# TensorE's wait before the gate and up products of a mixture of experts, split in two

## The chip, the cores and the metric

The kernel runs on one core of one Trainium2 chip, as one program. The metric is the device time of one execution in microseconds. Engines are named as the profile names them: PE is TensorE's products, PEld its weight loads, DVE is VectorE, ACT is ScalarE, POOL is GpSimd, SP is SyncE, which here only issues transfers. Each engine works through a queue of its own, in order, and the engines meet over semaphores.

## The reference

Two layers work on x of 4 x 1024 x 128 (float32). Layer 0 is a linear attention and a mixture of 8 experts with a capacity of 640 tokens each; layer 1 is a causal attention with cosine weights (16 heads of 64) and a mixture of 16 routed and 2 shared experts. What matters here is the mixture of layer 0:

```
disp = tokens scattered to [8 experts, 640 slots, 128]
h    = silu(disp @ W1) * (disp @ W2)        # gate and up, 128 -> 512, per expert
out  = h @ W3                               # down, 512 -> 128, per expert
y    = the two chosen experts' rows of each token, weighted and added
```

## The kernel before, in words

The program has four stages: layer 0's attention and routing, layer 0's experts, layer 1's attention, layer 1's mixture. The change is in the second.

**Half blocks.** For each expert the hidden width of 512 is cut into four blocks m of 128, and the 640 slots into two halves of 320. A half block is one (m, half); an expert has 8, numbered n = 0 to 7, and through all experts j = 8e + n, 0 to 63. For each half block TensorE makes a gate product and an up product, each [128, 320] from three matmuls in a row (weights and slots are split into a high and a low part of type fp32r, and high x high, high x low and low x high are added in PSUM). They go to banks 2(n % 2) and 2(n % 2) + 1: gate to bank 0 or 2, up to bank 1 or 3. So a bank is used again two half blocks on.

**Who reads the banks.** ScalarE waits for the gate product (`e_gate`), and also for VectorE's product of half block j - 2 (it overwrites that half of `e_sg`), reads the gate bank through SiLU, writes `e_sg` and counts the semaphore `e_sg` up. VectorE waits for `e_sg` and `e_up`, reads the up bank, multiplies the two into `e_hs` and counts `e_h` up. In the last expert the result goes to the tile that the profile calls sb_h.

**The order on TensorE** is written out in `experts_tensor` (L1195): for an expert e of 1 to 6 it is half blocks 0 and 1; the transposes of expert e + 1's slots (`slots_tensor`, L1177); the down product of expert e - 1 (`down_tensor0`, L1252, 20 products in 40 passes); half blocks 2 to 7. Expert 0 has the transposes before its half block 4 and no down product; expert 7 has the down products of ten single tiles in three groups (`tiles_tensor`, L1273). Before a half block with half = 0 TensorE waits for the split weights (`e_ws`), before half block 0 for the transposed slots (`e_xT`).

**The order beside it.** ScalarE copies the down products out (L1329, L1330, then a drain) ahead of the activation of half block 2, and rounds the next expert's weights to the high part (L1288) behind odd half blocks. VectorE makes the low parts (L1294), the split of the turned slots (L1367, L1375) behind half block 1 (5 in expert 0), and the lists of rows (L1382 to L1387) at the end of an expert. GpSimd scatters each expert's outputs to DRAM (L1163). SyncE loads weights and slots two experts ahead: `experts_sync` issues W3 (L1098) when the down product of the expert before is done, and right behind it W1, W2 (L1093, L1094) and the slots (L1103).

Of the kernel before, what the change touches and what calls it, by code (L numbers as in the profile page):

```python
# [76 lines left out]
class Kernel:  # L77
# [1117 lines left out]
    def experts_tensor(self):  # L1195
        pe, S, bank = self.pe, self.S, self.bank
        three = ((0, 0), (0, 1), (1, 0))
        self.first_slots_tensor()
        for e in range(E0):
            i, last = e % 2, e == E0 - 1  # L1200
            for n, (m, half) in enumerate(self.jobs(e)):
                j = 2 * NB * e + n
                if not last and n == 2 * self.slots_at(e):
                    self.slots_tensor(e + 1)
                if last:
                    self.tiles_tensor(n)
                elif e and n == 2:
                    self.down_tensor0(e - 1)
                if half == 0:
                    pe.wait_ge(S["e_ws"], NB * e + m + 1)  # L1210
                if n == 0 or (e == 0 and n == 1):
                    pe.wait_ge(S["e_xT"], e + 2 if e else half + 1)
                cols = slice(half * HC, (half + 1) * HC)
                pe.wait_ge(S["e_h"], max(0, j - 1))
                for w, name in enumerate(("e_gate", "e_up")):
                    for k, (wp, xp) in enumerate(three):
                        ins = pe.matmul(bank[2 * (n % 2) + w][:, 0:HC], self.ews[:, i, wp, w, m * P:(m + 1) * P],  # L1217
                                        self.xeT[:, i, xp, cols], start=(k == 0), stop=(k == 2))
                    ins.then_inc(S[name], 1)
        self.tiles_tensor(2 * NB)  # L1220
# [1479 lines left out]
```

## Time and profile before

| what | us |
|---|---|
| runs of the kernel, median of 3 | 871.64 |
| lowest and highest of them | 871.23, 872.01 |
| profiled execution, its span | 873.5 |
| PE busy in the span | 817.3 (94%) |
| DVE, ACT, POOL busy | 614.8, 432.0, 394.9 |

The span reaches from the first to the last instruction of one profiled execution. A row of the order of time reads: start, length, engine, line, operation, out<-in, count, and in brackets how long the engine had been idle before it and for whom. Matmuls overlap, so the length of a row of many is not their sum. Times of start are from the span's beginning; the experts' stage lies between about 166 and 272 us.

### The profile page before, as it was taken

What the parts mean: (1) busy time and instruction counts of PE and PEld (TensorE: products, weight loads), DVE (VectorE), ACT (ScalarE), POOL (GpSimd) and SP (SyncE); (2) the same over time, 40 slices, a digit from 0 to 9 for tenths busy, and PEclk for the clock granted to TensorE, in tenths of its full rate; (3) what the DMA queues carried; (4) which work ended last, traced back from release to release, by engine and by line L of the source; (5) the groups of instructions that cost most, each with busy time, mean ns of one, the idle gap of its engine ahead of it and who ended that gap; (6) DMA issues with size and microseconds to landing.
All of it is one profiled execution on the core that took longest, in us unless ns stands there. A gap on an engine that the chain in (4) does not pass through costs nothing.

```text
span 873.5 us, 32577 instructions
## 1 busy us (share of the span) xinstructions
PE 817.3 (94%) x13678; PEld 704.8 (81%) x13678; DVE 614.8 (70%) x1775; ACT 432.0 (49%) x944; POOL 394.9 (45%) x399
## 2 busy tenths in 40 slices
PE   6999985699997899999999999999999999999998
PEld 5777854588996688888888888888888888878887
DVE  7888885575664775675777785876876776858875
ACT  6556532544343755555556465565564464433322
POOL 4358877224454653644545654457442342500000
PEclk9999995599998999999999999999999999999999
DMA  9714100524322100000100100100000000027761
GB/s 292 252 63 160 37 26 11 175 76 128 94 76 84 31 27 4 27 3 3 51 3 3 29 3 3 53 3 4 4 3 3 5 3 3 4 57 148 157 125 40
DMA packets 67905, 49.66 MB, mean 57 GB/s; under 512 B 5298, under 2 KB 62785, under 8 KB 67377
## 3 DMA queue, kind: packets, MB, share of 16 engines
q1 hardware_dynamic: 64288, 42.41, 18.1%
q0 software_dynamic: 3328, 5.16, 1.8%
q8 instruction: 109, 1.79, 0.8%
q14 instruction: 36, 0.29, 0.1%
q10 hardware_dynamic: 144, 0.02, 0.0%
HBM read 33.20 MB, written 16.10 MB: 56 GB/s over the span
## 4 chain that ended last, share of the span: by engine, by line
PE 78%; DVE 7%; issue 5%; POOL 4%; ACT 3%; DMA 2%; SPq 0%; ACTq 0%; POOLq 0%; DVEq 0%
PE psum L1531 11%; PE psum L1636 8%; PE psum L1663 7%; PE psum L1614 7%; PE psum L2294 5%; PE psum L1217 5%; PE psum L1566 5%; PE psum L1595 5%; PE psum L2312 4%; PE psum L1651 3%; PE psum L1577 3%; PE psum L1549 3%; PE psum L1252 3%; POOL disp L307 3%; DMA sb_e_x<-disp 1%
## 5 line engine op out<-in xcount | busy, mean ns | idle before, releaser
L2192 POOL TENSOR_TENSOR sb_a_qr<-sb_h,sb_a_csq 128x512 f32<-128x512 f32 x64 | 81.4, 1294 | 113.8 <-PE psum L1636 107.9
L2192 POOL TENSOR_TENSOR sb_a_qr<-sb_a_qp,sb_a_csq 128x512 f32<-128x512 f32 (+1 forms) x64 | 72.2, 1151 | 116.4 <-PE psum L1636 116.4
L1531 PE MATMUL psum<-sb_wkv,sb_a_hs 128*128 128x512 f32 x384 | 122.5, 428 | 1.0 <-ACT sb_a_hs L1982 0.7
L1790 ACT ACTIVATE sb_a_vr<-sb_a_va,sb_consts 128x520 f32<-128x520 f32 x128 | 86.4, 725 | 5.0 <-DVE sb_a_va L2052 4.3
L307 POOL DMA_INDIRECT disp<-sb_h,sb_slot x64 | 67.8, 1060 | 25.5 <-issue 17.6
L1531 PEld LDWEIGHTS psum<-sb_wkv,sb_a_hs 128*128 128x128 f32 x384 | 63.8, 191 | 13.0 <-ACT sb_a_hs L1982 0.9
L1636 PE MATMUL psum<-sb_a_vr,sb_a_kb 64*64 64x130 f32 x1920 | 72.7, 277 | 1.6 <-issue 1.6
L2073 DVE TENSOR_TENSOR sb_a_mid<-psum,sb_a_state 128x130 f32<-128x130 f32 x112 | 47.4, 424 | 36.2 <-PE psum L1636 36.1
L1163 POOL DMA_INDIRECT chosen<-sb_m_h3t,sb_e_row x40 | 39.4, 985 | 70.9 <-ACTq L1331 55.2
L1614 PE MATMUL psum<-sb_a_mid,sb_a_qr 64*64 64x65 f32 x2048 | 70.7, 218 | 0.0
L1217 PE MATMUL psum<-sb_e_xt,sb_e_ws 128*128 128x320 f32 x384 | 64.8, 324 | 4.5 <-DVE sb_e_hs L1411 3.7
L1767 ACT ACTIVATE sb_h<-psum,sb_cols 128x512 f32<-128x512 f32 x32 | 22.0, 687 | 90.7 <-PE psum L1566 90.7
L1217 PEld LDWEIGHTS psum<-sb_e_xt,sb_e_ws 128*128 128x128 f32 x384 | 59.1, 196 | 8.2 <-issue 5.1
L1663 PE MATMUL psum<-sb_a_wo,sb_a_ot 128*128 128x128 f32 x512 | 65.5, 281 | 0.0
L1614 PEld LDWEIGHTS psum<-sb_a_mid,sb_a_qr 64*64 64x64 f32 x2048 | 65.1, 134 | 0.0
L1636 PEld LDWEIGHTS psum<-sb_a_vr,sb_a_kb 64*64 64x64 f32 x1920 | 56.8, 132 | 9.9 <-issue 4.7
L1614 PE MATMUL psum<-sb_a_state,sb_a_qr 64*64 64x65 f32 x1792 | 62.7, 218 | 0.0
L2294 PE MATMUL psum<-sb_m_hs,sb_wgus 128*128 128x512 f32 x240 | 60.9, 401 | 0.7 <-DVE sb_m_hs L2427 0.7
L1663 PEld LDWEIGHTS psum<-sb_a_wo,sb_a_ot 128*128 128x128 f32 x512 | 59.6, 192 | 1.7
L2370 ACT ACTIVATE sb_m_sg<-psum 128x512 f32<-128x512 f32 x40 | 23.9, 598 | 71.3 <-PE psum L2294 70.5
L1614 PEld LDWEIGHTS psum<-sb_a_state,sb_a_qr 64*64 64x64 f32 x1792 | 57.9, 134 | 0.0
L2052 DVE TENSOR_TENSOR sb_a_va<-psum,sb_rows 128x512 f32<-128x512 f32 x64 | 44.0, 688 | 16.0 <-PE psum L1531 16.0
(283 smaller groups left out, 1947.4 us busy)
## 6 DMA issues: line engine op xcount, KB each, us to landing
sb_h<-turned SPq DMA_DIRECT2D x32, 256.0 KB, 5.5
sb_e_w<-in_w SPq DMA_DIRECT2D x24, 256.0 KB, 3.2
chosen<-sb_empty SPq DMA_DIRECT2D x8, 512.0 KB, 6.3
sb_a_g<-chosen SPq DMA_DIRECT2D x12, 256.0 KB, 3.5
disp<-sb_empty SPq DMA_DIRECT2D x4, 650.0 KB, 9.9
sb_e_x<-disp SPq DMA_DIRECT2D x7, 325.0 KB, 5.4
sb_a_wo<-in_wo SPq DMA_DIRECT2D x4, 512.0 KB, 4.8
out<-sb_x SPq DMA_DIRECT2D x7, 256.0 KB, 4.0
```

What stands on the lines that cost most here:

```text
L307: g.indirect_dma_start(out=self.disp, out_offset=bass.IndirectOffsetOnAxis(ap=self.slot[:, k, n:n + 1], axis=0), in_=self.H2[:, n, :], in_ ...
L1217: ins = pe.matmul(bank[2 * (n % 2) + w][:, 0:HC], self.ews[:, i, wp, w, m * P:(m + 1) * P], self.xeT[:, i, xp, cols], start=(k == 0), stop ...
L1531: ins = pe.matmul(self.values_bank(i) if kv else self.bank[0], hs[:, part, at:at + P], self.Wkv[ws][:, h, w], start=(k == 0), stop=(k == 2))
L1566: ins = pe.matmul(self.bank[2], self.Wq[ws][:, j // PH, (j % PH) * P:(j % PH + 1) * P], hs[:, part, :], start=(k == 0), stop=(k == 2))
L1614: ins = pe.matmul(self.bank[4 + q][c * DH:(c + 1) * DH, j * 65:(j + 1) * 65], Qr[p, k, j, r * DH:(r + 1) * DH], states[r][p, j, k, :], sta ...
L1636: ins = pe.matmul(self.bank[bk][q * DH:(q + 1) * DH, at:at + 130], Kb[t, 2 * j + q, :], Vr[t, 2 * j + q, :, :].rearrange("p k d -> p (k d) ...
L1663: ins = pe.matmul(self.bank[1][:, 0:D], self.oT1[:, m, :], self.Wog[b % 2][:, m, :], start=(m == 0), stop=(m == HD // P - 1))
L1790: ins = act.activation(self.Vr[i % 2][:, :, k, :], self.Va[i % 3][:], ACT.Copy, scale=self.c[("cos1", "sin1")[k]][:, n:n + 1])
L2052: v.tensor_tensor(self.Va[i % 3][:, :, 0:DH], self.values_bank(i).rearrange("p (h d) -> p h d", d=DH), self.c["bv1"][:, h * 512:(h + 1) * ...
L2073: ins = v.tensor_tensor(part(mid), first, part(state), ALU.add)
L2192: ins = g.tensor_tensor(self.Qr[i % 2][:, k, :, t], qp, rows(self.csQ[:, k, c * P + t.start:(c + 1) * P], PH), ALU.mult)
L2294: ins = pe.matmul(self.hidden_bank(t, w), self.Wgus[wp][:, w, blk * P:(blk + 1) * P], hs[:, xp, :], start=(n == 0), stop=(n == 2))
```

## The change

Before, a half block's six matmuls stood behind one wait: VectorE's product of half block j - 2 (`e_h` at j - 1). Now the gate's three matmuls wait for ScalarE's activation of half block j - 2 (`e_sg` at j - 1), and the up's three for VectorE's product of j - 2 (`e_h` at j - 1). Nothing else in the program is changed.

```diff
                 cols = slice(half * HC, (half + 1) * HC)
-                pe.wait_ge(S["e_h"], max(0, j - 1))
-                for w, name in enumerate(("e_gate", "e_up")):
+                for w, (name, free) in enumerate((("e_gate", "e_sg"), ("e_up", "e_h"))):
+                    pe.wait_ge(S[free], max(0, j - 1))
                     for k, (wp, xp) in enumerate(three):
                         ins = pe.matmul(bank[2 * (n % 2) + w][:, 0:HC], self.ews[:, i, wp, w, m * P:(m + 1) * P],
                                         self.xeT[:, i, xp, cols], start=(k == 0), stop=(k == 2))
```

## Rows read from the trace of the kernel before

**Rows 1.** The page: the chain that ended last, by engine
```profile
PE 78%; DVE 7%; issue 5%; POOL 4%; ACT 3%; DMA 2%; SPq 0%; ACTq 0%; POOLq 0%; DVEq 0%
```

**Rows 2.** Busy time by windows (start:end, length, engines): experts, then layer 1
```profile
166.00:272.00 106.00, 101.19 (x727) 97.31 (x728) 63.22 (x135) 43.59 (x114) 42.42 (x40) 0.97 0.36 111
285.00:800.00 515.00, 505.89 (x11704) 434.51 (x11704) 366.79 (x984) 281.00 (x622) 240.57 (x237) 1.00 0.08 18
```

**Rows 3.** Waits of TensorE, 160 to 300 us: in total, times, longest
```profile
PE psum L1217 <- DVE sb_e_hs L1411: 3.7, 7, 1.2
```

**Rows 4.** Order of time, TensorE's products
```profile
178.08 1.99 PE L1217 MATMUL psum<-sb_e_xt,sb_e_ws 128*128 128x320 f32 x12 [1.21 <-DVE sb_e_hs L1411]
...
184.84 2.00 PE L1217 MATMUL psum<-sb_e_xt,sb_e_ws 128*128 128x320 f32 x12
187.26 5.77 PE L1217 MATMUL psum<-sb_e_xt,sb_e_ws 128*128 128x320 f32 x36 [0.41 <-DVE sb_e_hs L1411]
192.87 0.71 PE L1177 MATMUL psum<-sb_consts,sb_e_x 128*128 128x128 f32 x5
...
200.21 5.77 PE L1217 MATMUL psum<-sb_e_xt,sb_e_ws 128*128 128x320 f32 x36 [0.41 <-DVE sb_e_hs L1411]
```

**Rows 5.** Chain in order of time (start, length, what), up to 187.26
```profile
186.09 0.45 ACT sb_e_sg L1315
...
186.62 0.50 DVE sb_e_hs L1411
187.12 0.14 issue
```

**Rows 6.** Order of time, TensorE's products in windows of a few hundredths
```profile
186.54 0.31 PE L1217 MATMUL psum<-sb_e_xt,sb_e_ws 128*128 128x320 f32 x1
...
188.07 0.46 PE L1217 MATMUL psum<-sb_e_xt,sb_e_ws 128*128 128x320 f32 x2
...
188.95 0.31 PE L1217 MATMUL psum<-sb_e_xt,sb_e_ws 128*128 128x320 f32 x1
...
189.15 0.53 PE L1217 MATMUL psum<-sb_e_xt,sb_e_ws 128*128 128x320 f32 x2
```

**Rows 7.** Order of time, expert 7, VectorE and the weight load behind it
```profile
267.34 0.49 DVE L1411 TENSOR_TENSOR sb_h<-psum,sb_e_sg 128x320 f32<-128x320 f32 x1 [4.87 <-ACT sb_e_sg L1315]
...
267.89 0.19 PEld L1217 LDWEIGHTS psum<-sb_e_xt,sb_e_ws 128*128 128x128 f32 x1
```

**Rows 8.** Line L1214: wait instructions that stand by themselves, ns min/median/max
```profile
L1214 PEldq EVENT_SEMAPHORE  x33: 51/51/1793, 164.3 to 259.0; - x33
```

**Rows 9.** Order of time, VectorE before the stall of 178.08
```profile
176.38 0.82 DVE L1375 TENSOR_TENSOR sb_e_xt<-psum,sb_e_xt 128x640 fp32r<-128x640 f32 x1
...
177.45 0.48 DVE L1411 TENSOR_TENSOR sb_e_hs<-psum,sb_e_sg 128x320 f32<-128x320 f32 x1
```

**Rows 10.** Order of time, SyncE's issues and the transposes that wait
```profile
186.56 0.43 SPq L1103 DMA_DIRECT2D sb_e_x<-disp  x1
198.07 0.38 SPq L1098 DMA_DIRECT2D sb_e_w<-in_w  x1
...
206.29 0.76 PE L1177 MATMUL psum<-sb_consts,sb_e_x 128*128 128x128 f32 x5 [0.32 <-DMA sb_e_x<-disp]
```

**Rows 11.** Chain in order of time, the slots' transfer
```profile
199.52 6.73 DMA sb_e_x<-disp
```

**Rows 12.** Tile sb_e_x: its transfers
```profile
DMA to landing us min/median/max: 2.6/5.3/6.7
```

**Rows 13.** Order of time, SyncE's load and TensorE's first products of layer 1
```profile
268.78 0.90 SPq L1490 DMA_DIRECT2D sb_m_h3t<-chosen  x2
...
277.52 0.41 PE L1957 MATMUL psum<-sb_consts,sb_a_xn 128*128 128x128 f32 x2 [4.01 <-ACT sb_a_xn L1949]
```

**Rows 14.** Busy time by windows: after the engines come clock, DMA share, GB/s
```profile
277.50:281.00 3.50, 2.82 (x9) 1.97 (x10) 1.45 (x3) 0.56 (x1) 1.17 (x4) 0.58 0.32 92
281.00:285.00 4.00, 4.00 (x17) 3.49 (x16) 3.45 (x12) 2.41 (x5) 0.29 (x1) 0.51 0.77 224
```

## The prediction

> **What bounds the kernel now.** I read the chain of waits first: TensorE's products are 78% of the path that ended last, and every other engine is under 8% [rows 1]. Then the windows by stage: in the experts' stage (166 to 272 us of the trace) TensorE is busy for 101.19 of 106 us, in the attention and mixture behind it for 505.89 of 515 us [rows 2]. So time saved here has to be idle time of TensorE, and what is saved should reach the end, because the stage behind is bound by the same engine. Third, the waits of TensorE. The line that the change touches (L1217, gate and up products) waited for VectorE's product 3.7 us in all, 7 times, 1.2 us at the longest; so it is the products of L1217, not those behind them, that the engine is late for [rows 3]. The order of time shows where the 7 are: one before the first half block of expert 1 (178.08), and one in each of experts 1 to 6 before their fifth half block, such as 187.26 with 0.41 us idle [rows 4].
>
> Why the fifth: between the second and third half blocks stand 40 down passes of the expert before. ScalarE must first copy their results out, so it starts the activation of the third half block only at 186.09. The chain then reads activation 0.45, VectorE's product 0.50 to 187.12, 0.14 to the first gate product of the fifth half block at 187.26 [rows 5]. That gate product writes the bank that the activation has read out by 186.54; it waits for a product that reads another bank.
>
> **The change, part by part.** It adds no arithmetic, no transfer and no buffer. It moves one wait and adds one on TensorE's queue alone.
>
> *Gate products wait for ScalarE.* At the stall of 187.26 the last up product of the fourth half block started at 186.54. An unhindered crossing into an even half block goes from 188.95 to 189.15 in 0.20 us [rows 6]. Hence the stall costs 0.72 - 0.20 = 0.52 us over a crossing that has to be paid anyway. The activation is done at 186.09 + 0.45 = 186.54 [rows 5], before TensorE could start at 186.54 + 0.20 = 186.74. So the three gate products start at about 186.74 and occupy, at the starts of 188.07 and its successor (two starts with 0.15 between them: two products span 0.46, one takes 0.31), 0.15 each, with about 0.08 more behind the first after such a crossing: 0.52 in all, to 187.26.
>
> *Up products keep waiting for VectorE, now by themselves.* What waits here holds up all that is behind it on TensorE: this half block's up products and the next half block's. VectorE's product ends at 187.12 [rows 5]. A weight load that carries such a wait on itself started at 267.89 after a VectorE product that ended at 267.34 + 0.49 = 267.83, 0.05 later [rows 7]. Here that is 187.17, against 187.11 when the load would start unhindered. I take 0.02 us of the 0.06 as lost, so the stall shrinks by about 0.50 us. The next waits are not late: the activation of the fourth half block ends at most one activation (0.45) behind that of the third, which is one half block of TensorE's time early, and the product two half blocks back is always older than the one that now releases the gate.
>
> *The added wait when nothing is late.* Now each half block has a wait for VectorE in front of its gate products. The trace has 33 separate wait instructions at L1214 for 64 half blocks [rows 8]: about every second wait stands by itself, where the wait for split weights shares the spot, and the others ride on a weight load. The half block whose gate starts at 188.21 is of the second kind and starts 0.15 after the product ahead, as products inside a group do [rows 6]. The new wait in front of an up load is alone there, so I take zero. The other end: a separate instruction, which costs the crossing of 0.20 against 0.15 and a first product that holds its successor for 0.23 instead of 0.15, 0.13 us together, times 62 (two waits are for zero). That is 8.1 us. Below nothing is excluded, since no wait makes a product shorter.
>
> *The first stall, 178.08.* Here VectorE is late with more: it splits the turned slots of expert 1 until 176.38 + 0.82 = 177.20, which the gate also needs, and ends the product waited for at 177.45 + 0.48 = 177.93 [rows 9]. The gate products now start at about 177.20 + 0.15 = 177.35 and end at 177.87; the up load starts at 177.93 + 0.05, products at about 178.05 instead of 178.08 + 0.52 = 178.60. That is 0.5 us of the 1.2; the rest stays.
>
> *What eats one of them: the slots' transfer.* The slots for the expert after next are sent for only when the down products are done: from 198.07 on SyncE issues weight loads, at 199.52 the slots, and that transfer took 6.73 us, so TensorE sits idle for 0.32 us before the transposes of 206.29 [rows 10, 11]. Its distance from the down products does not depend on TensorE's stall between them. So the 0.50 won at 200.21 turns into a longer wait at 206.29: gain zero. For the others: slots issued at 186.56, needed at 192.87 [rows 4, 10], 6.31 us; after the change 5.8. The transfers of slots landed in 2.6 to 6.7, median 5.3 us [rows 12], 0.5 us of slack at the median, and only the one of 199.52 made the transposes wait. Expert 6's stall has no transposes behind it.
>
> *Expert 7* has no such stall: its down passes stand elsewhere, and nothing changes there. The way from the last half block into the attention runs over ScalarE's copies, GpSimd's scatters and the load that SyncE issues behind their landing at 268.78, until TensorE starts again at 277.52 after 4.01 us idle [rows 13]. Each of these waits for the one before and the first for TensorE, so the whole passage moves by the same amount.
>
> **Sum:** stalls in experts 1, 3, 4, 5 and 6: 5 x 0.50 = 2.5; the first 0.5; expert 2's 0. Together 3.0 us. In the profiled execution the span goes from 873.5 to 870.5. The runs shown have a median of 871.64, 1.9 us less than that span; I carry the difference over: 868.6 us.
>
> **Rivals.**
> *A, the transfer isn't late next time (chance 0.12).* Its window also held a slower weight load, so it may be a chance event. Then expert 2's 0.50 and the present idle 0.32 with its restart (0.1 to 0.2) come too: 4.0 us, 867.6.
> *B, the transfers become the bound (0.03).* Four more transfers stand behind a stall that goes (those needed in experts 2, 4, 5 and 6). If all landed after 6.7 us instead of 5.3, their transposes would come 6.77 after the issue instead of 6.31: 4 x 0.46 = 1.8 slower, less 1.0 for the first stall and expert 6's: +0.8, 872.4. Slower than before from a landing time of 6.5 on. For it: one did so. Against: load and spacing stay the same relative to each other.
> *C, each up wait costs a separate instruction (0.03).* 8.1 - 3.0 = +5.1: 876.7. It decides from 0.05 us a wait on. It is the case in which the change ends slower than before. Against it stand the 33 for 64 [rows 8] and the crossing at 188.21.
> *D, the low clock at the start of attention falls elsewhere (0.10).* After 4 us without TensorE work the granted clock is 0.58 and then 0.51, near the lower of its two levels (half of 2.4 GHz), over 277.5 to 285, in which TensorE is busy for 2.82 + 4.00 = 6.82 us [rows 14]. Nearly all of it is on the path. If the low stretch missed the work: 3.4 us more gain, 865.2 (0.04). If it lasted as long again: 3.4 us lost, 872.0 (0.06). The three runs of before lie within 0.8 us, which speaks against either, and the idle time ahead of it stays as long. The Trainium skill (TensorE: Matmul & The Clock Gate, Part 1: The HAM clock gate) says that the moment of the change of clock varies from run to run of the same kernel, as it isn't tied to the kernel's start. By that the shift of 3 us alone would change nothing systematic; a single execution can't show it.
> *E, it is given back inside the stage (0.04).* Were the next half block stopped by its up wait, the time would only move. For it: VectorE has slot splits and weight splits behind the second half block. Against: these lie under the 40 down passes. Then 871.6.
>
> **How the numbers follow.** The forecast has 0.68: 868.6, with its own range 868.0 to 869.4 (0.45 to 0.52 a stall, and one transfer more that eats 0.5). What a measurement here tells from no change is 0.2%, 1.7 us: faster is below 869.9. Faster: 0.68 + 0.12 (A) + 0.04 (D down) = 0.84; within: 0.06 (D up) + 0.04 (E) + 0.02 (most of B) = 0.12; slower: 0.04 with C and the rest of B. The range reaches to A below and to two or three late transfers above: 867.2 to 870.1.
>
> **What would show it.** In the waits of the changed kernel, L1217 for VectorE falls from 3.7 us in 7 to about 0.3 in one or two, and there is hardly a wait of L1217 for ScalarE. The fifth half block follows the fourth without idle time, so 12 + 36 products stand as one group of 48. The period of the experts, 12.95 us between the stalls of 187.26 and 200.21 [rows 4], falls to about 12.45, except the one with the late transfer, where the idle time before the transposes grows from 0.3 to 0.8. The wait instructions stay at 33 or so; 95 would be C. Transposes with idle time before them in three or more experts would be B. The attention starts 3 us earlier; if it does and the end doesn't, the clock row of its first 8 us decides.

## The result, and the profile after

| | median, us | lowest to highest | runs |
|---|---|---|---|
| kernel before | 871.42 | 871.14 to 872.01 | 5 |
| changed kernel | 866.82 | 865.25 to 867.58 | 5 |

The ratio is 0.9938, with a 95% interval from 0.9927 to 0.9948. By the medians the change saves 4.6 us, by the ratio 4.5 to 6.4. The forecast was 868.6, with a range from 867.2 to 870.1; the direction held, the gain was larger than the 3.0 us foreseen, and the median lies 0.4 us below the range.

The page of the changed kernel gives a span of 864.3 us for an execution of 865.63. Its chain that ended last, by engine, answers to [rows 1]:

```profile
span 864.3 us, 32577 instructions
...
PE 79%; DVE 8%; issue 5%; POOL 4%; ACT 3%; DMA 1%; POOLq 0%; SPq 0%; DVEq 0%; ACTq 0%
```

TensorE bounds it as before. The waits of TensorE between 160 and 300 us (in total, times, longest) no longer hold the line of [rows 3]; all that is left of L1217 is this:

```profile
PE psum L1217 <- issue: 1.4, 2, 0.9
```

The 0.9 stands before the first product of expert 0, where the kernel before has 0.6 (*before_again*, below); the other 0.56 is what is left of the first stall.

The order of time on TensorE answers to [rows 4]:

```profile
170.03 3.77 PE L1217 MATMUL psum<-sb_e_xt,sb_e_ws 128*128 128x320 f32 x24
174.35 2.27 PE L1217 MATMUL psum<-sb_e_xt,sb_e_ws 128*128 128x320 f32 x12 [0.56 <-issue]
176.47 0.71 PE L1177 MATMUL psum<-sb_consts,sb_e_x 128*128 128x128 f32 x5
...
181.40 7.43 PE L1217 MATMUL psum<-sb_e_xt,sb_e_ws 128*128 128x320 f32 x48
...
193.59 7.42 PE L1217 MATMUL psum<-sb_e_xt,sb_e_ws 128*128 128x320 f32 x48
...
205.78 7.43 PE L1217 MATMUL psum<-sb_e_xt,sb_e_ws 128*128 128x320 f32 x48
213.13 0.77 PE L1177 MATMUL psum<-sb_consts,sb_e_x 128*128 128x128 f32 x5
```

The stall before the fifth half block is gone: 12 and 36 products have become one group of 48, without idle time. The period, from 181.40 to 193.59, is 12.19 us, where 12.45 was forecast and 12.95 stood before.

To know what of this belongs to the change and what to one execution, the kernel before was profiled once more (*before_again*, span 870.8 us, against 873.5 of the first trace). Its order of time:

```profile
171.17 3.89 PE L1217 MATMUL psum<-sb_e_xt,sb_e_ws 128*128 128x320 f32 x24
176.27 1.99 PE L1217 MATMUL psum<-sb_e_xt,sb_e_ws 128*128 128x320 f32 x12 [1.21 <-DVE sb_e_hs L1411]
178.10 0.71 PE L1177 MATMUL psum<-sb_consts,sb_e_x 128*128 128x128 f32 x5
...
185.44 5.78 PE L1217 MATMUL psum<-sb_e_xt,sb_e_ws 128*128 128x320 f32 x36 [0.41 <-DVE sb_e_hs L1411]
191.06 0.71 PE L1177 MATMUL psum<-sb_consts,sb_e_x 128*128 128x128 f32 x5
...
198.40 5.78 PE L1217 MATMUL psum<-sb_e_xt,sb_e_ws 128*128 128x320 f32 x36 [0.41 <-DVE sb_e_hs L1411]
204.01 0.71 PE L1177 MATMUL psum<-sb_consts,sb_e_x 128*128 128x128 f32 x5
```

The reader is to see two things. The stalls of 0.41 and 1.21 us come back unchanged, so they are the kernel's. And the transposes at 204.01 have no idle time before them: the late slots of [rows 10, 11] were an event of one execution.

**Where the time went.** Subtracting *before_again* from the changed kernel, with the starts of rows: the experts from the first product of expert 1 to the first down product of expert 7 take 75.48 us instead of 79.53, so 4.05 less; expert 0 with the first stall takes 9.92 instead of 10.53, so 0.61 less. That is 4.66 us in the stage that was changed. The spans differ by 6.5 us. Of the remaining 1.8, 1.3 us lie ahead of the first gate product, and 0.5 behind the experts, where the two programs are the same. A second profile of the changed kernel (*again2*, span 864.9) has 0.9 and 1.3 there, 4.09 in experts 1 to 6, and 0.41 more time, not less, in expert 0. These are differences between executions. Two of them show in the clock. Windows from 262 to 285 us, which hold the start of the attention, in *before_again*:

```profile
262.00:285.00 23.00, 17.79 (x104) 15.31 (x104) 10.88 (x31) 9.51 (x23) 10.42 (x15) 0.85 0.35 103
```

The same window in the first profile of the changed kernel:

```profile
262.00:285.00 23.00, 16.17 (x116) 12.88 (x117) 14.93 (x40) 11.37 (x26) 7.75 (x11) 0.93 0.31 87
```

and in its second:

```profile
262.00:285.00 23.00, 16.14 (x113) 12.79 (x111) 13.79 (x36) 10.39 (x25) 8.71 (x12) 0.85 0.33 95
```

The figure behind the busy times is the granted clock: 0.85, 0.93, 0.85. And 168 to 171 us, in expert 0 of the first profile and then of *again2*:

```profile
168.00:171.00 3.00, 3.00 (x24) 2.99 (x23) 2.50 (x8) 1.42 (x4) 0.00 (x0) 1.00 1.05 361
```

```profile
168.00:171.00 3.00, 3.00 (x15) 3.00 (x14) 1.73 (x6) 1.04 (x4) 0.00 (x0) 0.58 1.01 357
```

With 1.00 the changed kernel gets 24 products into 3 us, with 0.58 only 15: that is the expert 0 of *again2*. The same kernel was granted more in one execution than in another. The Trainium skill (TensorE: Matmul & The Clock Gate, Part 1: The HAM clock gate) says that the moment of the change varies from run to run of one kernel; by that rule, the traces agree.

### The profile page after: what moved, and what is told of

It is laid out like the page before. It is cut to its first block, busy times and chain, and to the rows that moved or that the text cites. A ratio compares the mean times of both kernels' runs of the same rounds, so it can differ in the third digit from the quotient of the medians.

```text
span 864.3 us, 32577 instructions
## 1 busy us (share of the span) xinstructions
PE 810.9 (94%) x13678; PEld 700.3 (81%) x13678; DVE 610.2 (71%) x1775; ACT 431.8 (50%) x944; POOL 396.0 (46%) x399
## 4 chain that ended last, share of the span: by engine, by line
PE 79%; DVE 8%; issue 5%; POOL 4%; ACT 3%; DMA 1%; POOLq 0%; SPq 0%; DVEq 0%; ACTq 0%
PE psum L1531 11%; PE psum L1636 8%; PE psum L1663 7%; PE psum L1217 7%; PE psum L1614 7%; PE psum L2294 5%; PE psum L1595 5%; PE psum L1566 5%; PE psum L2312 4%; PE psum L1651 3%; PE psum L1577 3%; PE psum L1549 3%; PE psum L1252 3%; POOL disp L307 3%; POOL sb_l_y L231 1%
## 5 line engine op out<-in xcount | busy, mean ns | idle before, releaser
L1663 PE MATMUL psum<-sb_a_wo,sb_a_ot 128*128 128x128 f32 x512 | 65.5, 281 | 0.0
L1217 PE MATMUL psum<-sb_e_xt,sb_e_ws 128*128 128x320 f32 x384 | 61.6, 319 | 1.4 <-issue 1.4
L1663 PEld LDWEIGHTS psum<-sb_a_wo,sb_a_ot 128*128 128x128 f32 x512 | 59.6, 192 | 1.7
L1217 PEld LDWEIGHTS psum<-sb_e_xt,sb_e_ws 128*128 128x128 f32 x384 | 57.9, 193 | 3.1 <-issue 2.0
```

Source lines behind the costliest of these rows:

```text
L1663: ins = pe.matmul(self.bank[1][:, 0:D], self.oT1[:, m, :], self.Wog[b % 2][:, m, :], start=(m == 0), stop=(m == HD // P - 1))
```

## What was to be explained

One theory, L: the crossing of 0.20 us into an even half block [rows 6], which the prediction took as a cost that has to be paid, is itself a wait. A gate product waits for VectorE's product of two half blocks ago. This chain is a loop: six products of gate and up, then VectorE's product, then the next gate but one; and it is longer than two half blocks of TensorE's own work. One turn of it goes from the fifth half block's first gate product at 187.26 to the seventh's at 189.15, 1.89 us; twelve products at the 0.147 us between starts inside a group make 1.76. In the first trace VectorE's product of the fifth half block reads

```profile
188.51 0.49 DVE L1411 TENSOR_TENSOR sb_e_hs<-psum,sb_e_sg 128x320 f32<-128x320 f32 x1 [1.00 <-ACT sb_e_sg L1315]
```

It ends at 189.00, and the gate product of the seventh starts at 189.15 [rows 6], 0.15 later, which is the same distance as from 187.12 to 187.26 at the stall [rows 5]. In the changed kernel the same crossing is this row (a window of a few hundredths):

```profile
184.99 0.46 PE L1217 MATMUL psum<-sb_e_xt,sb_e_ws 128*128 128x320 f32 x2
```

Two products in 0.46 us, of which one takes 0.31, are 0.15 apart: the first is the last up product of the sixth half block, the second, at 185.14, the first gate product of the seventh, and it doesn't wait. Against 0.20 before, plus the 0.08 by which the first product behind such a wait holds up its successor, that is 0.13 us a crossing. There are two such crossings an expert (into the seventh half block, and into the first of the next expert). The rivals were that the stalls alone had been mis-sized, that the added waits do something, and that the rest is the clock (theory K in the expectations) or the transfers.

The traces at hand answer the clock. Over the same 60 us in the experts, first *before_again*, then the changed kernel:

```profile
185.00:245.00 60.00, 57.96 (x429) 55.72 (x429) 38.78 (x79) 25.30 (x67) 30.34 (x28) 1.00 0.41 121
185.00:245.00 60.00, 60.00 (x460) 59.01 (x459) 37.30 (x85) 26.21 (x69) 30.70 (x28) 1.00 0.39 116
```

Both were granted 1.00 throughout, and the changed kernel gets 31 more products into the stretch. Over whole executions the mean granted clock was 0.973 in the 23 runs of the kernel before and 0.973 in the 6 of *again2* on one chip, at medians 4.6 us apart. So the gain isn't the clock's. Nor is it the transfers': *before_again* has no late transposes, and its periods are 12.95 us all the same.

## The experiments

Kernels that are listed together ran on one chip and share the runs of the kernel before. The periods are the distances between the groups of L1217 behind the down products of one expert and the next, for experts in which no transposes were late.

| kernel | median, us | ratio to before, with interval | period, us |
|---|---|---|---|
| before, first chip of the study | 886.1 (879.9 to 888.7) | | |
| again | 884.66 | 0.9998 [0.9969, 1.0027] | 12.19 |
| stalls_only | 885.85 | 0.9997 [0.9971, 1.0022] | 12.45 |
| rest_only | 884.83 | 0.9993 [0.9968, 1.0017] | 12.70 |
| own_waits | 900.36 | 1.0179 [1.0148, 1.0210] | 12.36 |
| before, second chip | 871.59 (869.92 to 873.57) | | |
| before_again | 871.48 | 1.0002 [0.9992, 1.0012] | 12.95 |
| again2 | 866.95 | 0.9951 [0.9933, 0.9968] | 12.19 |
| copies_later | 867.04 | 0.9944 [0.9927, 0.9962] | 12.05 |
| copies_before | 869.88 | 0.9982 [0.9969, 0.9994] | 12.66 |
| before, third chip | 872.03 (870.55 to 872.98) | | |
| slow_vector_before | 872.29 | 1.0008 [0.9999, 1.0018] | 13.17 |
| slow_vector | 868.11 | 0.9955 [0.9942, 0.9968] | 12.28 |
| best | 865.20 | 0.9927 [0.9915, 0.9940] | 12.05 |
| own_waits2 | 881.29 | 1.0110 [1.0095, 1.0124] | 12.19 |
| before, fourth chip | 884.4 (880.9 to 888.1) | | |
| stalls_only2 | 884.16 | 0.9985 [0.9961, 1.0010] | 12.45 |
| rest_only2 | 884.11 | 0.9985 [0.9961, 1.0008] | 12.69 |
| best2 | 879.25 | 0.9947 [0.9921, 0.9973] | 12.05 |

Of *before_again*, L had expected the period of 12.95, which came; a late transfer again, and some 8 us of idle time without a releaser in the experts' stage, expected by two other theories, didn't (0.6 us). Of *again2*, L had expected 75.5 to 75.7 us from the first product of expert 1 to the first down product of expert 7; it took 75.44.

### again, stalls_only, rest_only: the two halves of the change

*again* is the changed kernel once more.

> The changed kernel once more, for its time on the chip of the next three and for a second trace. All theories: 0.5% below the kernel before (866.8 against 871.4 us). Theory P (the prediction's): a stall costs 0.52 us over an inherent crossing of 0.20, and the slots' transfer usually eats one; that makes 3.0 us. Theory L (loop): each even half block waited for VectorE's product in a loop that is longer than TensorE's own two half blocks, so six experts save 0.52 + 2 x 0.13 = 0.78 us each, 4.7 us. Theory K (clock): the part above 3 us is where the low clock falls; then the traces differ in the low stretches near 165 and 275 us, and the time moves by 1.7 us for each of about 3.4 us of low clock over busy products. Under L the period of the experts is 12.2 us in every trace, whatever the clock does.

*stalls_only* splits the wait at the half blocks that stalled, and nowhere else:

```diff
+                split = n == 4 or (e, n) == (1, 0)
                 for w, (name, free) in enumerate((("e_gate", "e_sg"), ("e_up", "e_h"))):
-                    pe.wait_ge(S[free], max(0, j - 1))
+                    if split or w == 0:
+                        pe.wait_ge(S[free if split else "e_h"], max(0, j - 1))
```

> Only the fifth half block of each expert, and the first of expert 1, have the two waits; all others wait for VectorE before the gate as before. Theory P: nothing else is ever late, so this is as fast as the changed kernel (-4.6 us or what again shows). Theory L: the even half blocks 6 and 0 still wait in the loop, 0.13 us each, 12 of them: 1.5 us slower than the changed kernel, -3.1 us against before, a period of 12.45 us. Theory K: as P.

*rest_only* is its complement: `split = not (n == 4 or (e, n) == (1, 0))`.

> The opposite: the fifth half block of each expert and the first of expert 1 wait as before, all others have the two waits. Theory P and K: no gain, within 0.2 us of before. Theory L: the loop's 12 x 0.13 = 1.5 us go, the seven stalls stay: -1.5 us, a period of 12.7 us with 0.4 us idle at the fifth half block.

The times don't tell the parts apart: on this chip even the changed kernel is level with the one before. That is more than spread, since the interval of *again*, from 0.9969, lies wholly above that of the first result, up to 0.9948: here the gain of the stage didn't reach the end. Its twelve runs were granted a mean clock of 0.965, the 29 of the kernel before 0.968. As an estimate from these means, with half the clock at the lower level, that is some 5 us more at the lower level and up to 2.7 us of time; why it was so is open. What the times lack the traces have. First the waits of *again*, whose L1217 stood idle for 8.0 us where the same program had 1.4 on the other chip, and no releaser is seen (the chip of the first profile isn't on record; its times are those of the faster chips):

```profile
PE psum L1217 <- issue: 8.0, 3, 4.5
```

Where none of these disturbances and no late transposes fall, the rows repeat to 0.01 us. The order of time of *stalls_only*:

```profile
196.20 7.69 PE L1219 MATMUL psum<-sb_e_xt,sb_e_ws 128*128 128x320 f32 x48
...
208.65 7.69 PE L1219 MATMUL psum<-sb_e_xt,sb_e_ws 128*128 128x320 f32 x48
```

and of *rest_only*:

```profile
192.66 2.00 PE L1219 MATMUL psum<-sb_e_xt,sb_e_ws 128*128 128x320 f32 x12
195.08 5.51 PE L1219 MATMUL psum<-sb_e_xt,sb_e_ws 128*128 128x320 f32 x36 [0.42 <-DVE sb_e_hs L1413]
...
205.36 2.00 PE L1219 MATMUL psum<-sb_e_xt,sb_e_ws 128*128 128x320 f32 x12
```

The stalls alone give 208.65 - 196.20 = 12.45, 0.50 under 12.95. The rest alone keeps the stall at 0.42 and gives 12.70, 0.25 less, although no row of the kernel before showed an idle time there: its 36 products take 5.51 us instead of 5.78. The two parts sum to 0.75 of the 0.76. So the second part is real. Single starts show that it lies at the crossings: the last up product of the sixth half block and the first gate product of the seventh, in *stalls_only* and then in *rest_only*:

```profile
199.79 0.59 PE L1219 MATMUL psum<-sb_e_xt,sb_e_ws 128*128 128x320 f32 x2
```

```profile
196.76 0.46 PE L1219 MATMUL psum<-sb_e_xt,sb_e_ws 128*128 128x320 f32 x2
```

The first pair starts 0.20 us apart (199.79 and 200.00), the second 0.15 (196.76 and 196.91). *stalls_only2* and *rest_only2*, the same two kernels on another chip, were to settle it in time as well.

> The kernel stalls_only once more, since its first time came with idle stretches of several us of no releaser. L: 12.45 us a period; the seven stalls alone are 3.5 of 4.9 us, so 868.2 where before takes 871.6 (-3.4, ratio 0.996), 1.3 us above the changed kernel. P: as fast as the changed kernel, 867.0.

> The kernel rest_only once more for the same reason. L: 12.69 us a period, -1.4 us, 870.2 (ratio 0.9984). P: no gain.

They repeat the periods, 12.45 and 12.69. In *stalls_only2* TensorE stood idle before two groups of transposes (periods of 13.27 and 13.87); late slots are likely, but the profile names no releaser. This chip, like the first, takes 884 us for the kernel before, and the times don't tell the parts apart (both 0.9985, with intervals that hold 1). The gains expected in time, 3.4 and 1.4 us, did not show. How the 4.6 us divide is shown by the traces alone.

### own_waits and own_waits2: what a separate wait costs

Rival C's price. In front of each up product a further wait is put that is satisfied long before:

```diff
                     pe.wait_ge(S[free], max(0, j - 1))
+                    if w:
+                        pe.wait_ge(S["e_ws"], NB * e + m + 1)
```

> The changed kernel with one more wait before each up product, for the split weights, which are long there. It makes the wait for VectorE or this one an instruction of its own, 64 times. Rival C of the prediction: 0.13 us each, +8 us against the changed kernel. Theory L says that the 0.13 us seen at a separate wait was the loop's lateness and not the instruction: TensorE's queue runs through a satisfied wait ahead of the products, so +0.0 to 0.5 us.

> The kernel own_waits once more (the changed kernel with one more satisfied wait before each up product), beside runs without the idle stretches of the first four. In its first run the experts cost only 0.16 us a period more, but attention and mixture, which have the same instructions, took 15 us longer, with idle time of TensorE before L1665 and L1653 that ends with no releaser. Theory F: TensorE's instructions reach it in pieces, and 62 more of them shift the pieces' edges into dense products; then the 15 us come again on any chip. Theory N (that chip's trouble): here it is 0.5 to 1 us above the changed kernel, 867.5.

The trace of *own_waits2* lists the added wait as an instruction of its own, before all 64 up products:

```profile
L1217 PEldq EVENT_SEMAPHORE  x64: 51/51/51, 165.0 to 261.3; - x64
```

In the stage itself these 64 instructions cost little or nothing: the period of *own_waits2* is 12.19, that of the changed kernel; on the first chip it was 12.36, 0.17 more for eight of them, where rival C's 0.13 us each would be 1.0. But the kernel is 9 us slower than the one before (ratio 1.0110) and 14 slower than the changed one, and not in this stage: from TensorE's first product of the attention to the end it takes 609.0 us, where *again2* takes 594.5. The program is the same there. The waits of TensorE in the whole of *own_waits2* show where:

```profile
PE psum L1665 <- issue: 6.7, 10, 1.6
PE psum L1653 <- issue: 2.9, 7, 0.8
```

These are lines L1663 and L1651 of the other kernels, moved by two. In *again2* the first has no such wait, and the second has this:

```profile
PE psum L1651 <- issue: 0.8, 1, 0.8
```

So 8.8 of the 14.5 us stand as idle time without a releaser before two lines of the attention. In time neither C's +8 us nor L's +0.5 came but +14 to +16 against the changed kernel, on both chips, as theory F said. That the engine waits there for its instructions, F's mechanism, is only inferred; no run varies it.

### copies_later and copies_before: what is left of the fifth half block

ScalarE's copies of the down products move from ahead of the third activation to ahead of the fifth, in the changed kernel and in the one before:

```diff
-                elif e and n == 2:
+                elif e and n == 4:
                     self.outputs_scalar0(e - 1)
```

> The changed kernel, with ScalarE's two copies of the down products moved from ahead of the activation of half block 2 to ahead of that of half block 4. The activation of half block 2 then starts 0.9 us earlier, so that the up product of half block 4 finds VectorE's product long done (it lost 0.08 us by it). L: the period falls by that 0.08 us to 12.10, 0.5 us over six experts, not to be told in the time; GpSimd's scatters start 1.9 us later, hidden. If the copies hold up half block 4's activation instead, the up product of half block 6 is late and the period rises.

> The kernel before (one wait for VectorE before the gate) with the same move of the copies. L: the stall of 0.52 us at the fifth half block goes without any split of the wait, since the activation and VectorE's product of half block 2 come 0.9 us earlier; but then the loop over VectorE binds at half block 4 as at 6 and 0, 0.13 us each, and the copies (0.9 us in ScalarE's queue) delay the activation of half block 4 by about 0.9, which stalls half block 6 by 0.4 to 0.8 instead. Period 12.7 to 12.95. If the crossing cost of 0.13 us were inherent (P), the changed kernel's period could not be 12.2, and this one would be 12.45.

*copies_later* in order of time:

```profile
182.93 7.29 PE L1217 MATMUL psum<-sb_e_xt,sb_e_ws 128*128 128x320 f32 x48
...
194.98 7.28 PE L1217 MATMUL psum<-sb_e_xt,sb_e_ws 128*128 128x320 f32 x48
```

The period is 12.05, so 0.14 less than the changed kernel's: that is what its two waits still cost at the fifth half block. The changed kernel's own trace divides it (windows of a few hundredths, first the gate, then the up products of one such half block):

```profile
183.24 0.52 PE L1217 MATMUL psum<-sb_e_xt,sb_e_ws 128*128 128x320 f32 x2
```

```profile
183.74 0.54 PE L1217 MATMUL psum<-sb_e_xt,sb_e_ws 128*128 128x320 f32 x2
```

A product takes 0.31, so the second gate product starts at 183.45, 0.21 behind the first, and the second up product at 183.97, 0.23 behind the first, where 0.15 is the distance inside a group: 0.06 and 0.08. The gate's weight load starts at 183.20, 0.11 behind the end of ScalarE's activation, and the up's at 183.72, 0.05 behind the end of VectorE's product. So the gate, too, is still a little late, for ScalarE. The prediction had 0.08 behind the gate, 0.02 of lateness at the up product, and a restart there at nothing. In time the 0.14 can't be seen: 867.04 against 866.95 of *again2*. The period expected was 12.10.

In *copies_before* the first stall stays (1.2 us) and the others go out of the list of waits, yet the period is 12.66, not 12.05 (L had expected 12.7 to 12.95, P 12.45). The trace shows why, on VectorE and on TensorE's loads:

```profile
185.75 0.49 DVE L1411 TENSOR_TENSOR sb_e_hs<-psum,sb_e_sg 128x320 f32<-128x320 f32 x1 [0.74 <-ACT sb_e_sg L1315]
...
186.36 3.65 PEld L1217 LDWEIGHTS psum<-sb_e_xt,sb_e_ws 128*128 128x128 f32 x24 [0.35 <-issue]
```

The activation that now stands behind the copies is the fifth, so VectorE's product of the fifth half block ends at 186.24, and the first gate load of the seventh follows at 186.36 after 0.35 idle: the stall has moved two half blocks on and shrunk. By the starts of single products it now takes 0.35 of the 0.6; the other two crossings into even half blocks, the fifth and the next expert's first, take 0.13 each (184.07 to 184.28 at the fifth, and 0.08 behind it). Here the time follows the trace: six periods shorter by 0.29 are 1.7 us, and the medians differ by 1.7 (871.59 and 869.88).

### slow_vector: lengthening VectorE's step

A small operation, which writes to a tile that nothing reads, is put ahead of VectorE's product, behind its waits, in both kernels. If a crossing waits for VectorE, every crossing pays.

```diff
+                v.tensor_scalar(self.room[:, 5 * j:5 * j + 5], self.c["iota8"][:, 0:5], 0.0, 1.0, ALU.not_equal, ALU.mult)
```

> The kernel before, with one more VectorE instruction (128x5, 0.17 us alone, about 0.2 us in a row of dependent waits) between the arrival of a half block's operands and its product, 64 times. Theory L: TensorE waits in the loop over VectorE at the fifth half block and at the even crossings 6 and 0, so each of the three grows by 0.2 us: period 12.95 + 0.6 = 13.55 us, 3.7 us in all. Theory P (only the fifth half block waits, the crossing costs 0.20 by itself): period 13.15, 1.4 us in all.

> The same added instruction in the changed kernel. L: only the up product of the fifth half block still finds VectorE's product late (by 0.08 us of start to start), so it alone grows: period 12.19 + 0.2 = 12.4 us, at most 12.45, 1.4 us in all; at the other up products VectorE has 0.4 us to spare. If splitting the wait had only shifted the loop and not taken it out, the period would grow by 0.6 here too.

Order of time on VectorE, *slow_vector_before*:

```profile
186.99 0.17 DVE L1411 TENSOR_SCALAR sb_e_room<-sb_consts 128x5 f32<-128x5 f32 x1 [0.32 <-ACT sb_e_sg L1315]
187.07 0.48 DVE L1412 TENSOR_TENSOR sb_e_hs<-psum,sb_e_sg 128x320 f32<-128x320 f32 x1
```

and on TensorE:

```profile
184.86 5.92 PE L1217 MATMUL psum<-sb_e_xt,sb_e_ws 128*128 128x320 f32 x36 [0.49 <-DVE sb_e_hs L1412]
...
198.03 5.91 PE L1217 MATMUL psum<-sb_e_xt,sb_e_ws 128*128 128x320 f32 x36 [0.49 <-DVE sb_e_hs L1412]
```

The product starts 0.08 us behind the operation of 0.17: the two overlap, so the dose was 0.08 and not the 0.2 expected, and all sizes expected were too large for that reason (periods of 13.55 and 12.4, measured 13.17 and 12.28). The places count. The stall grows by 0.08 (0.41 to 0.49), and the 36 products behind it by 0.14 (5.78 to 5.92), at crossings without any listed idle time; the one into the seventh half block goes from 0.20 to 0.28 (186.55 to 186.82). The period grows by 0.22, about three times the dose. The changed kernel, in order of time:

```profile
183.63 7.50 PE L1217 MATMUL psum<-sb_e_xt,sb_e_ws 128*128 128x320 f32 x48
...
195.91 7.50 PE L1217 MATMUL psum<-sb_e_xt,sb_e_ws 128*128 128x320 f32 x48
```

Here it grows by 0.09, once the dose, at the one place where up still waits late. Three places to one is what L says; under P the kernel before would have grown at one place too. The medians can't show it: *slow_vector_before* lies 0.3 us above before, with an interval from -0.1 to +1.6, where six periods longer by 0.22 make 1.3.

### best and best2: more of the same

*best* is *copies_later* with expert 1's slots split earlier in expert 0:

```diff
-        return 1 if e else 2
+        return 1
...
-                if e + 1 < E0 and n == (1 if e else 5):
+                if e + 1 < E0 and n == (1 if e else 3):
```

*best2* is *copies_later* with SyncE issuing the slots ahead of the weights (`load_slots(e + 2)` before the loads of W1 and W2).

> A candidate that beats both: the changed kernel with ScalarE's copies later (copies_later), and expert 1's slots transposed before half block 2 of expert 0 and split behind its half block 3 instead of 4 and 5, so that VectorE's split is done before half block 0 of expert 1. L: the last of the first stall goes, 0.56 us ahead of the gate and 0.28 ahead of the up: 0.8 us below copies_later, 866.2, 5.4 us below before, unless the slots of expert 1 land later than the half block 2 begins. From the first to the last product of expert 0 and on to expert 1: no idle time but the crossing.

> A candidate: the changed kernel, copies later, and SyncE issues the slots ahead of W1 and W2 (about 1 us earlier), so that no transposes find them late. That takes 0 to 0.6 us of lateness that single traces show in one or two experts. Periods of 12.05 us in all experts. Time 866.4, within 0.2% of copies_later (867.0), so only the trace can tell; -5.2 us against before. If W1 and W2 come late instead, ScalarE's rounding behind half block 1 is held up and the activations behind it with it.

*best* in order of time:

```profile
173.38 3.35 PE L1217 MATMUL psum<-sb_e_xt,sb_e_ws 128*128 128x320 f32 x21 [0.81 <-DVE sb_e_hs L1411]
...
201.28 0.77 PE L1177 MATMUL psum<-sb_consts,sb_e_x 128*128 128x128 f32 x5 [0.44 <-DMA sb_e_x<-disp]
```

The first stall only moved into expert 0, with 0.81 us, and one transfer of slots was late by 0.44. So the expectation's mechanism failed, though the time, 865.2, even lies below the 866.2 expected. The 865.2 us lie under both kernels, but the interval, 0.9915 to 0.9940, overlaps the changed kernel's. In *best2* no slots were late in the one profile (periods of 12.04 to 12.06); one profile doesn't show that the order did it, and it ran on the chip that takes 884 us for the kernel before. Its median is 5.2 us below that, as expected.

## Why the prediction was wrong in size

**Right.** TensorE bounds the stage, and on the faster chips what its waits lose comes back at the end. The stall before the fifth half block gave 0.50 us an expert, as worked out (12.95 to 12.45 in *stalls_only*). That this figure came out is partly luck: the prediction left 0.05 for a crossing over the pitch of a group, 0.08 behind the gate and 0.02 at the up product, 0.15 together; the changed kernel has 0, 0.06 and 0.08, which is 0.14. The crossing counted too long made up for the restart counted at nothing. The added wait rides along: 33 separate wait instructions after as before, and the crossing into the seventh half block at a plain 0.15. Rival C needed 0.05 us a wait; *own_waits2* found none in the stage, for waits that stand by themselves. Rivals B and E didn't come. Rival D, the clock, differs from execution to execution (0.93 and 0.85 above), but not between the kernels' means on one chip.

**The step that failed** is the sentence "An unhindered crossing into an even half block goes from 188.95 to 189.15 in 0.20 us", and with it "0.52 us over a crossing that has to be paid anyway". The crossing was hindered. The row in the order of time showed no idle time, since a gap of 0.05 us lies within the modelled length of the product before it (0.31); but the product of VectorE that releases the crossing ended 0.15 us ahead of it, as at the stall. I took the smallest distance that the kernel showed at this kind of place for its floor, while the distance of 0.15 inside a group stood beside it. Two crossings in each of experts 1 to 6 are 6 x 0.26 = 1.56, and one of expert 0 (the group of 24, 3.89 to 3.77 us) 0.12: together 1.7 us that the sum didn't have.

**Expert 2's 0.** The sum gave expert 2 nothing because of the late slots. This was rival A, at a chance of 0.12, and *before_again* shows that it was right: the lateness belonged to one execution. That is 0.5 us more. But the shorter stretch between issue and need, which the prediction worked out, may still cost a little, which is not shown by an experiment: *before_again* has no period above 12.96, the changed kernel's two profiles have 12.34, 12.26 and 12.39 where 12.19 is the plain one, together 0.2 us in each, and *best* has one transfer late by 0.44.

**The first stall** gave less than the 0.5 worked out. From the group of 24 in expert 0 to the transposes in expert 1, *before_again* has 171.17 to 178.10 = 6.93 us, the changed kernel 170.03 to 176.47 = 6.44. That is 0.49, of which 0.12 is the crossing just counted: 0.37 for the stall.

**The sum again:** six stalls of 0.50, 3.0; the first 0.37; crossings 1.7; less some 0.2 for transfers a little late: 4.9 us. It lies within both intervals (4.5 to 6.4, and 2.8 to 5.8 by *again2*), and near the 4.6 of both pairs of medians. The difference to 3.0 is explained; that the medians say 4.6 and not 4.9 is less than these runs resolve. On the first chip of the study the sum isn't borne out in time, as said above.

**The span.** The forecast carried over a difference of 1.9 us between the first trace's span and the median. *before_again* shows why it was there: an execution runs 1.3 us longer than its span (872.15 for 870.8), so the first trace was an unusually long one. Carrying the difference over was sound.

## What to carry to other kernels

The shortest distance seen between two instructions at a kind of place isn't the floor of that place: compare it with the distance inside a group, and with the end of what releases it, before it is called free. Where a buffer of depth two links engines in a ring, add up one turn of the ring; if it is longer than the bottleneck's own work for two steps, each turn loses the difference, in pieces too small to be listed as idle time. And before a single late transfer is put into a sum, profile the kernel a second time.

## What the runs showed of the hardware beside it

- 64 wait instructions that never wait cost next to nothing where they stand (12.19 us a period without them, 12.19 and 12.36 with them), and 14 us in the next stage, as idle time without a releaser at instructions that are the same in both programs. It came on two chips. No experiment told what it depends on.
- On two of the four chips of the study the kernel before took 884 to 886 us instead of 872, spread over 7 to 9 us; the profiles taken there have single idle stretches of up to 4.8 us without a releaser. A gain of half a per cent showed there for *best2* (0.9921 to 0.9973) and not for *again* (0.9969 to 1.0027); undisturbed periods inside the stage were the same as on the faster chips to 0.01 us, but for *own_waits*.
- A VectorE operation of 0.17 us on 5 columns delayed the product behind it by 0.08 us only.
